# Last down projection in two column halves, one transpose for a half of the softmax companion, and W_o's maximum taken one token block earlier

## What is computed

```python
xn = layernorm(x)                                  # no affine part
q, k, v = heads(xn @ Wq.T), heads(xn @ Wk.T), heads(xn @ Wv.T)   # 16 heads of 32
q, k = rope(q), rope(k)
attn = softmax(causal(q @ k.T / sqrt(32)))         # 512 x 512 for each head
s = merge(attn @ v) @ Wo.T
h = gelu(bitlinear(xn, w_fc))                      # 512 -> 2048, exact gelu
g = silu(bitlinear(h, w_proj))                     # 2048 -> 512
out = x + s * g

def bitlinear(x, w):       # ternary weights, one scale; x normalised over its features first
    x = (x - mean(x)) / sqrt(var(x) + 1e-6)
    x = clip(x * 128 / gamma, -128, 128) * gamma / 128    # gamma = max |x|; no rounding
    return x @ (sign(round(w / (mean|w| + 1e-6))) * mean|w|).T
```

## Time and profile before

| | us |
|---|---|
| median of 3 runs | 1116.93 |
| lowest and highest | 1116.35 and 1117.47 |
| the profiled execution, its time | 1117.98 |
| its span, first to last instruction | 1116.3 |
| PE busy | 1087.4 |
| DVE, ACT, POOL busy | 865.5, 771.7, 519.8 |
| mean granted TensorE clock | 0.997 of full |

### The profile page before, as it was taken

How to read it: one execution, slowest core, us unless ns; L and a number is a source line. 1 busy time by engine, 2 the same in 40 slices (tenths; PEclk the granted TensorE clock), 3 DMA queues, 4 the chain that set the end, 5 groups by cost and what they waited for, 6 DMA issues and landing times.

```text
span 1116.3 us, 19950 instructions
## 1 busy us (share of the span) xinstructions
PE 1087.4 (97%) x7404; PEld 595.0 (53%) x7404; DVE 865.5 (78%) x1623; ACT 771.7 (69%) x1478; POOL 519.8 (47%) x915
## 2 busy tenths in 40 slices
PE   4999998999999999999999999999999999999998
PEld 3565653447544584446734475444844467444763
DVE  6986975899758987589766997579874898668964
ACT  4797983379835898269862798448982688727984
POOL 2035361374625637165352745247371663626533
PEclk9999998999999999999999999999999999999999
DMA  9494013851039202491026610493013910256101
GB/s 319 161 99 93 1 22 52 110 94 39 18 52 126 73 11 40 62 137 38 2 40 94 105 39 4 67 103 86 21 26 60 153 40 2 40 79 82 39 15 64
DMA packets 86401, 75.68 MB, mean 68 GB/s; under 512 B 43168, under 2 KB 68128, under 8 KB 85792
## 3 DMA queue, kind: packets, MB, share of 16 engines
q1 hardware_dynamic: 86304, 74.41, 37.0%
HBM read 31.98 MB, written 8.40 MB: 36 GB/s over the span
## 4 chain that ended last, share of the span: by engine, by line
PE 87%; DVE 5%; ACT 3%; DMA 2%; POOL 1%; issue 1%; SPq 1%; DVEq 0%; ACTq 0%; POOLq 0%
PE banks L450 20%; PE banks L585 19%; PE banks L630 14%; PE banks L711 7%; PE banks L692 6%; PE banks L564 6%; PE banks L467 5%; PE banks L641 4%; PE banks L571 2%; ACT banks L892 2%; PE banks L484 1%; PE banks L421 1%; DMA v_sb<-in_L_attn_Wv_dram 1%; DVE mix L1201 1%; DVE arena L1171 1%
## 5 line engine op out<-in xcount | busy, mean ns | idle before, releaser
L892 ACT ACTIVATE banks<-banks,mix,scl 128x384 f32<-128x384 f32 (+2 forms) x384 | 248.2, 649 | 21.0 <-POOL mix L1416 15.5
L1201 DVE TENSOR_REDUCE mix<-banks 128x1 f32<-128x512 f32 (+3 forms) x352 | 216.0, 637 | 27.7 <-PE banks L571 23.4
L585 PE MATMUL banks<-xT,fcT 128*128 128x512 f16 x1024 | 227.8, 379 | 2.3 <-ACT xh_buf L856 1.8
L630 PE MATMUL banks<-proj_ones,arena 128*128 128x256 f16 (+1 forms) x1536 | 213.3, 273 | 0.0
L1407 POOL TENSOR_TENSOR xh_buf<-xh_buf 128x512 f32<-128x512 f32 x120 | 152.4, 1270 | 68.0 <-ACT xh_buf L856 66.6
L915 ACT ACTIVATE arena<-banks,scl 128x1280 f32<-128x1280 f32 x128 | 162.1, 1330 | 30.1 <-PE banks L692 27.2
L450 PE MATMUL banks<-xT,qkT 128*128 128x512 f16 x768 | 170.7, 383 | 0.1
L585 PEld LDWEIGHTS banks<-xT,fcT 128*128 128x128 f16 x1024 | 98.5, 98 | 121.3 <-ACT xh_buf L856 6.0
L630 PEld LDWEIGHTS banks<-proj_ones,arena 128*128 128x128 f16 x1536 | 141.7, 97 | 35.9
L1416 POOL TENSOR_SCALAR mix<-mix,scl 128x1 f32<-128x1 f32 (+1 forms) x288 | 76.5, 266 | 174.2 <-DVE mix L1201 172.8
L1401 POOL TENSOR_TENSOR xh_buf<-xr_buf,xh_buf 128x512 f16<-128x512 f32 x32 | 37.0, 1176 | 217.0 <-ACT xh_buf L828 217.0
(11 more groups left out here) (165 smaller groups left out, 1418.2 us busy)
## 6 DMA issues: line engine op xcount, KB each, us to landing
stacks<-xh_buf SPq DMA_DIRECT2D x96, 128.0 KB, 5.2
stacks<-split_buf SPq DMA_DIRECT2D x96, 128.0 KB, 7.6
out_dram<-arena SPq DMA_DIRECT2D x32, 256.0 KB, 2.0
xr_buf<-in_L_attn_x_dram SPq DMA_DIRECT2D x7, 1024.0 KB, 11.2
resid<-in_L_attn_x_dram SPq DMA_DIRECT2D x28, 256.0 KB, 4.8
stacks<-in_L_ffn_w_fc_dram SPq DMA_DIRECT2D x1, 4096.0 KB, 26.0
arena<-in_L_ffn_w_proj_dram SPq DMA_DIRECT2D x1, 4096.0 KB, 15.3
mix<-norm_row SPq DMA_DIRECT2D x8, 256.0 KB, 4.5
```

What stands on the lines that cost most here:

```text
L585: mm = pe.matmul(banks[:, UP_BANKS[f % NUB], :], fcT[:, c, f * P:(f + 1) * P], xT[:, part, c, :], start=(c == 0 and part == 0), stop=(c == ...
L630: mm = pe.matmul(banks[:, DOWN_BANKS[h % 3], 0:cols.stop - cols.start], hid[:, part, f, t * P:(t + 1) * P], proj_ones[:, f, cols], start=( ...
L892: mm = nc.scalar.activation(block, block, ACT.Exp, scale=col(EXP_SCALE), bias=exp_bias[:, i, h0 + k:h0 + k + 1], accum_out=row_sum[:, i, h ...
L1201: nc.vector.tensor_reduce(row_max[:, i, h0:h0 + n], scores_of(r), AX_X, ALU.max).then_inc(max_ready, 1)
```

## The change

Four things change.

1. The fourth token tile of the down projection has its left half as a seventh step of `down()` (32 matmuls of 257 columns into bank 5, copied by ACT as the others), and its right half as 32 matmuls of 256 columns into bank 7. The 32 matmuls of one column go. The order of the tile halves' columns is now the same for all tiles. Five right-half matmuls stand ahead of `scores(0)`, behind them the sums of squares, and 27 beside the heads 0 to 4.
2. The companion's columns are ordered part, head, tile. A half is one transpose of 128x128 (96 columns are used) and not four; DVE copies 96 partitions of 128 columns and not 24 of 512, and the DMA reads as many bytes from 96 partitions.
3. DVE makes the remaining token statistics and the second half of the companion ahead of the reading of the sums, and reads these in two pieces. The centring of the fourth tile is two instructions of 256 columns, the right from bank 7, the left from SBUF.
4. `largest(3)` is called in body 0, behind `finish_context(2)`; `rope_rows(1)` behind `out_weights()` in body 1.

```diff
-DOWN_BANKS = (7, 5, 6)
-N_HALF = 2 * (NT - 1)
+DOWN_BANKS = (7, 5, 6, 7, 5, 6, 5)
+N_HALF = 2 * NT - 1
...
-DOWN_BESIDE_EXP = (3, 3, 3, 3, 2, 2)
+LAST_AHEAD = 5
+DOWN_BESIDE_EXP = (6, 6, 6, 5, 4)
...
                 def turn_lse(half, bank):
 
                     pe.wait_ge(lse_split, 2 * b + half + 1)
-                    for i in range(NT):
-                        at = (half * NT + i) * SPLITS * HH
-                        mm = pe.transpose(banks16[:, bank, i * P:(i + 1) * P], parts_f[:, at:at + P], ident16[:])
-                    mm.then_inc(maxT_ps, 1)
+                    at = half * SPLITS * HH * NT
+                    pe.transpose(banks16[:, bank, 0:P], parts_f[:, at:at + P], ident16[:]).then_inc(maxT_ps, 1)
...
-                            mm = pe.matmul(banks[:, 7, :], hid[:, part, f, S - P:S], projT[:, f, :],
+                            mm = pe.matmul(banks[:, 7, 0:D // 2], hid[:, part, f, S - P:S], projT[:, f, D // 2:D],
...
+                while given < ahead + N_HALF * FC:
+                    next(downs)
+                    given += 1
+                for _ in range(LAST_AHEAD):
+                    next(downs)
                 pe.wait_ge(down_kept, b * N_HALF + N_HALF - 1)
-                for f in range(FC):
-                    for part in range(2):
-                        pe.matmul(banks[:, 5, D // 2 + 1:D // 2 + 2], hid[:, part, f, S - P:S], ones16[:, 0:1],
-                                  start=(f == 0 and part == 0), stop=(f == FC - 1 and part == 1))
                 pe.wait_ge(sq_split, b * 4 + 4)
...
-                while given < ahead + NT * DOWN_MATMULS - sum(DOWN_BESIDE_EXP):
-                    next(downs)
-                    given += 1
...
                     if h == 1:
-                        pe.wait_ge(sums_read, 3 * b + 3)
+                        pe.wait_ge(down_kept, b * N_HALF + N_HALF)
...
                 exp_of_guess(1)
+                keep_down(N_HALF - 1)
                 for h in range(H):
...
             def out_weights():
-                largest(3)
                 scale_of(3, 3, 6, 1e-30)
...
-                nc.vector.tensor_copy(maxT[:, :], banks16[0:SPLITS * HH, bank, 0:S]).then_inc(maxT_ready, 1)
+                nc.vector.tensor_copy(maxT[:, :], banks16[0:SPLITS * HH * NT, bank, 0:P]).then_inc(maxT_ready, 1)
...
                 if b == 1:
                     out_weights()
+                    rope_rows(1)
...
-                centre(NT - 1, banks[:, 7, :])
+                right = slice(D // 2, D)
+                centre(NT - 1, banks[:, 7, 0:D // 2], right)
+                left = slice(0, D // 2)
+                centre(NT - 1, gate[:, NT - 1, left], left).then_inc(centred, 1)
...
                     finish_context(g)
+                    if g == 2 and first:
+                        largest(3)
...
-                if not last:
+                if not first and not last:
                     rope_rows(b + 1)
```

73 lines of the change are left out of this document (37 added, 36 removed).

## The result

The changed kernel takes 1108.51 us (median of 4 runs, 1108.03 to 1110.45), the kernel before, measured beside it, 1117.2: ratio 0.9926, 95% interval 0.9909 to 0.9943. It is faster, as forecast, but by 8.7 us and not by 13.4, and it ends above the range (1101.7 to 1107.5). It is set against the one of before, whose span was 1116.3: 9.6 us of span to explain.

The account below looks back on a forecast made before the run. It took TensorE's issue as the bound mid-program and a chain through VectorE at body 1's start. 8.5 us from the bodies plus 4.9 from W_o, 13.4 off 1117.98, gave 1104.6, 1103.5 as a median; range 1101.7 to 1107.5.

Parts of the forecast that it names:

- Ahead of T: Before T, the start of `scores(0)` in each body: 0.23 us less from the halves, 0.17 from the single transpose.
- T to the first weighing: From `scores(0)` to TensorE's first weighing: moves from T + 7.09 to T + 6.4, VectorE's companion copy just in time.
- T to the end of the heads: From `scores(0)` to V, the next batch's first value tile: 0.67 us less for a body.
- Who might be late instead: Check of other engines around the heads in each body: 0.05 us a body taken off for "just in time".
- W_o: Start of body 1: earlier maximum brings rotation products forward, a new 2.2 us wait before pair 3; gain 4.9 us, once.
- rival 1: Start of body 1: clock falls to half in the new wait, about 2.5 us more, 1106.0; chance 0.12.
- The sum: Whole kernel: 8.5 us from eight bodies and 4.9 from W_o, 13.4 us gained.
- Rival 2: Behind T: ScalarE's 1.24 us a head sets the pace, 5.8 us lost, 1109.3; chance 0.12, whole or good part.
- Rival 3: Companion's DMA in smaller pieces late for `scores(8)`: 1.7 us lost a body, 1118 to 1120; chance of slower 0.02.
- Rival 4: Start of body 1: new wait smaller as two splits run faster, up to 1.7 us better, 1101.8; chance 0.07.

Follow-up runs that it names:

- Halves alone: Changed kernel with four transposes and without W_o's part, leaving the fourth tile in halves and the order of statistics and sums: 1114.19 us, ratio 0.9973.
- the steps at (2, 3, 7, 8): Changed kernel with GpSimd's last four normalisation steps behind the masks of heads 2, 3, 7, 8 instead of 3, 4, 5, 6: 1106.61 us, ratio 0.9914.
- W_o's part alone: Kernel before with only W_o's maximum made in body 0 and body 1's rope rows behind the scale and first two splits: 1114.27 us, ratio 0.9974.
- the centring moved: Changed kernel with VectorE's centring of tiles 0 to 2 behind the first context instead of ahead of it: 1108.84 us, ratio 0.9931.
- the steps moved by less: Changed kernel with GpSimd's last four normalisation steps behind the masks of heads 2, 3, 4, 7 instead of 3, 4, 5, 6: 1106.33 us, ratio 0.9901.

## Why the prediction was wrong, point by point

- **Ahead of T: right.** 0.40 us for a body worked out, 0.41 measured. The price of a half step (0.110) held. The fixed 2.5 ns for a matmul, which the prediction drew from the Trainium skill, "TensorE: Matmul & The Clock Gate", "Wait — 56ns, not 53.3ns?", would be, as an estimate, 0.0075 us for three matmuls more; 0.67 for 0.66 is as near to it as to nothing, and it moves no term here.
- **T to the first weighing: right.** T + 6.4 worked out, T + 6.43 measured. The copy of the companion was taken at 0.25 and takes 0.22. Halves alone showed that this copy was indeed what stood next there: with 512 columns the weighing comes 0.24 us later than TensorE's own work allows.
- **T to the end of the heads: wrong, and this is the step that failed.** "Who might be late instead" went through ScalarE, VectorE's copy and the DMA, and left out GpSimd, which masks each exponential between ScalarE and TensorE. The gain of 0.67 at the first weighing was taken as kept to the end. From T to V the bodies 0 to 6 gave 0.28, 0.17, 0.38, 0.17, 0.16, 0.25 and 0.17 us, 1.6 in all and not 7 x 0.67 = 4.7. The missing 3.1 us went, nearly all, to waits for the masks. Moving two of GpSimd's steps brought nearly all of it back (T to V 20.81 in two kernels), so it is shown. The remark that VectorE's work there is something "which nobody on the path waits for" overlooks that masks beside it last longer; but taking it away alone gained nothing.
- **W_o: the mechanism right, the size off by the clock.** The maximum lies in VectorE's gap (at 170.88, "near 174" was written), the spread at 185.01 follows the first query product, and the new wait is 2.27 (2.2 worked out). The forecast held the clock at full, and it fell: rival 1, to which 0.12 was given. The price was 1.7 us, not 2.5, since the clock was low for 3.4 us and not for 5.1. The gain was 3.38 + 0.47 = 3.85 for 4.9; with the clock full the kernel with the steps at (2, 3, 7, 8) has 31.04 - 25.96 = 5.08, and only 0.04 more in its up projection. The prediction also misread the row on which rival 1 rests: TensorE was idle from 186.01, and the mean of 0.54 over the stretch from 189 puts the fall at 189.1, so the clock held for 3.1 us and not for 3.5. In the changed kernel it fell 2.7 us behind the start of the new wait, when work had already begun again.
- **The sum.** 13.4 worked out; less 3.1 for the masks and 1.05 for W_o, that is 9.2; body 0 gave 0.56 ahead of its T where 0.23 was counted, which makes 9.6, as the span has it. Of that 0.56, 0.43 are there at the first query product of body 0 and lie within the scatter of the start: luck, not a gain of the change. The profiled execution of before took 1117.98, 0.8 us above the 1117.2 of the comparison, and the one of after lay on its median, which is why the medians differ by 8.7 only.
- **Rival 2, ScalarE paces the heads:** did not happen. Its first ten exponentials take 12.86 us, 1.29 each, and TensorE's waits list none for them. The last body, where GpSimd has no steps, kept 0.67 of 0.72; there too masks beside the centring last up to 0.85 us each for 0.41 alone, but head 7's begins at T + 11.01 and not at T + 11.68.
- **Rival 3, the companion's DMA:** did not happen. With pieces of 256 B the last data came 0.1 us later behind the issue, within what the rows resolve, and `scores(8)` came 2 us behind the last data.
- **Rival 4, a smaller wait:** did not happen, 2.27 us.

## What to carry to other kernels

When work is taken from the engine that sets the pace, every engine between two of its steps must be costed in its queue, the quiet ones too: a queue that is never waited for may have a quarter of a microsecond to spare, and no bracket shows that. Work it out as (time at which the next instruction wants the result) less (time at which the trace has it). A stage that runs without the suspected work, like the last body here, tells in one comparison whether the rest of the gain is there.

## What the hardware showed that I had not expected

- The same idle time of TensorE has two outcomes. After 2.26 or 2.27 us without work the granted clock went to half in the profiles of the changed kernel, of W_o's part alone, of the centring moved and of the steps moved by less, and stayed at full in that of the steps at (2, 3, 7, 8). The runs of one kernel differ too (mean clock 0.998 in six runs of W_o's part alone, 1.000 in three). The fall costs 1.7 us in the query and key products, and 1.3 up to T. Which one a run gets is open.
- GpSimd slows beside VectorE's work on SBUF: a pair of masks 0.77 us alone, 0.95 to 1.48 beside the centring; a step on 4 columns 0.20 and 0.63. The kernel before shows it as well (1.45 and 0.63).
- One DMA of the same bytes in pieces of 256 instead of 1024 B was not measurably slower: last data 2.0 us behind the issue for 1.9.
